# Attention with a ring of four PSUM banks for exponentials and three single banks for maxima

## The reference

```
xd = (layernorm(x) @ W_down).reshape(b, t, 16, 16)
keys, queries, values = per-head 16x16 products of xd     # keys and queries times 16 ** -0.25
dot  = einsum('bqhs,bkhs->bhqk', queries, keys)
attn = softmax(dot, axis=-1)
out  = einsum('bhqk,bkhs->bqhs', attn, values).reshape(b, t, 256) @ W_unify + b_unify
```

## Time and profile before

| | |
|---|---|
| runs shown | 2726.8, 2732.42, 2734.16 us; median 2732.42 |
| the profiled execution | 2731.22 us, span 2729.5 us, mean granted clock 0.979 |
| TensorE (PE) matmuls, weight loads (PEld) | 2627.3 us (96%), 1574.4 us (58%) |
| VectorE (DVE) | 2021.7 us (74%) |
| ScalarE (ACT) | 1761.2 us (65%) |
| GpSimd (POOL) | 917.5 us (34%) |
| attention steps | from about 647 to 2138 us of the span |

### The profile page before, as it was taken

One profiled execution on the slowest core, in us unless ns is written; L12 is line 12 of the kernel. 1 busy time (PEld: TensorE's weight loads), 2 busy tenths in 40 slices (PEclk: granted clock), 3 DMA queues, 4 the chain that ended last, 5 costly groups with the idle time before them and its releaser, 6 DMA issues. The chain is left out here.

```text
span 2729.5 us, 45612 instructions
## 1 busy us (share of the span) xinstructions
PE 2627.3 (96%) x17009; PEld 1574.4 (58%) x17009; DVE 2021.7 (74%) x3407; ACT 1761.2 (65%) x3314; POOL 917.5 (34%) x975
## 2 busy tenths in 40 slices
PE   6999999968999999999999999999999699999998
PEld 5888899953334334333343343343333388888998
DVE  5656547848898898897988988978997266665586
ACT  4444456734787887877877878878778344444576
POOL 2333334641332242423323322422212133332364
PEclk9999999986999999999999999999999699999999
DMA  4421214515144243242342442432421331321253
GB/s 116 100 70 56 62 52 137 156 53 101 48 85 85 55 96 66 65 99 52 77 105 51 90 80 54 81 65 65 84 68 32 107 86 57 76 70 32 86 160 96
DMA packets 191805, 216.79 MB, mean 79 GB/s; under 512 B 56364, under 2 KB 152804, under 8 KB 191584
## 3 DMA queue, kind: packets, MB, share of 16 engines
q1 hardware_dynamic: 156176, 169.03, 26.6%
q0 software_dynamic: 35408, 44.84, 5.8%
HBM read 114.54 MB, written 48.57 MB: 60 GB/s over the span
## 5 line engine op out<-in xcount | busy, mean ns | idle before, releaser
L1383 DVE TENSOR_REDUCE at_mxc<-at_pb 128x2 f32<-128x1024 f32 x1024 | 1217.7, 1222 | 185.2 <-PE at_pb L1208 178.4
L1316 ACT ACTIVATE at_ex<-at_pd 128x512 f32<-128x512 f32 x2048 | 1074.1, 603 | 328.9 <-PE at_pd L1219 325.1
L1219 PE MATMUL at_pd<-at_qa,at_ka 50*128 50x512 f32 x2048 | 616.2, 471 | 4.4 <-ACT at_ex L1316 4.4
L1219 PEld LDWEIGHTS at_pd<-at_qa,at_ka 50*128 50x128 f32 x2048 | 271.2, 186 | 570.8 <-issue 410.2
L699 ACT ACTIVATE f_ml_h<-f_ml_pL,b1T 128x512 f32<-128x512 f32 (+1 forms) x384 | 243.2, 633 | 480.2 <-PE f_ml_pL L763 458.7
L1228 PE MATMUL at_po<-at_ex,at_va 128*32 128x512 f32 x4096 | 551.5, 611 | 0.0
L614 DVE TENSOR_TENSOR f_ml_hl<-f_ml_h,f_ml_hh 128x512 fp32r<-128x512 f32 (+1 forms) x384 | 277.9, 724 | 368.0 <-ACT f_ml_hh L702 335.1
L1208 PE MATMUL at_pb<-at_ka,at_qa 48*128 48x512 f32 x2048 | 412.0, 447 | 21.6 <-DMA at_ka<-at_parts 11.3
L776 PE MATMUL f_ml_pA<-f_wh,f_ml_hh 128*128 128x256 f32 (+1 forms) x1408 | 411.4, 292 | 0.0
L778 PE MATMUL f_ml_pA<-f_wl,f_ml_hh 128*128 128x256 f32 (+1 forms) x1408 | 396.8, 282 | 0.0
L779 PE MATMUL f_ml_pA<-f_wh,f_ml_hl 128*128 128x256 f32 (+1 forms) x1408 | 396.7, 282 | 0.0
(11 more groups left out here) (123 smaller groups left out, 2642.0 us busy)
## 6 DMA issues: line engine op xcount, KB each, us to landing
f_wraw<-in_L_ffn_w SPq DMA_DIRECT2D x128, 256.0 KB, 2.9
at_qa<-at_parts SPq DMA_DIRECT2D x384, 64.0 KB, 2.5
at_ka<-at_parts SPq DMA_DIRECT2D x384, 64.0 KB, 2.7
at_oscr<-at_os POOLq DMA_DIRECT2D x63, 256.0 KB, 2.4
f_ml_xr<-in_L_attn_x SPq DMA_DIRECT2D x16, 512.0 KB
f_ml_xs<-in_L_attn_x SPq DMA_DIRECT2D x16, 512.0 KB, 4.6
x<-f_ml_yo SPq DMA_DIRECT2D x16, 512.0 KB, 6.2
at_xr<-x SPq DMA_DIRECT2D x16, 512.0 KB, 5.3
```

The source lines that it names most:

```text
L1219: eng.matmul(pd[n % RING][:, :], ka[g][rows, p, kt * P:(kt + 1) * P], qa[g][rows, qh, p, :], start=True, stop=True).then_inc(s_full.sem, 1)
L1316: eng.activation(ex[t % 2][:, j, :], pd[n % RING][:, :], ACT.Exp).then_inc(s_free[n % RING].sem, 1)
L1383: eng.tensor_reduce(mxc[:, t // NT, kh, t % NT::NT], pb[kh][:, :].rearrange("p (e k) -> p e k", e=2), AX.X, ALU.max, negate=True).then_inc ...
```

## The change

The two double banks for maxima become one tensor of MRING = 3 banks, and the ring of the exponentials gets the eighth bank: RING = 4. A maxima tile is now 128 queries x 512 keys of one head. It has a running number n (tile_of_max), uses bank n mod 3, waits for the read of tile n - 3, and has its own reduce of 512 numbers, so a step has four tiles and four reduces where it had two. TensorE's order within a step stays as it was (ORDER is 0, 1, 2, 3, and the e loops run where the pairs stood). The setup of the diagonals uses the first two of the three banks.

```diff
-RING = 3
+RING = 4
+MRING = 3
+ORDER = (0, 1, 2, 3)
...
-        pb = [ps(f"pb{i}", [P, T]) for i in range(2)]
+        pb = ps("pb", [P, MRING * 512])
         pd = [ps(f"pd{i}", [P, 512]) for i in range(RING)]
...
+        def tile_of_max(b, g, t, kh, e):
+            return 4 * (ST * unit(b, g) + t) + 2 * kh + e
+
+        def bank_of_max(n):
+            return pb[:, n % MRING * 512:(n % MRING + 1) * 512]
...
-            def for_max(b, g, t, kh):
+            def for_max(b, g, t, kh, e):
...
-                eng.wait_ge(s_mx.sem, s_mx.at(2 * (ST * unit(b, g) + t) + kh - 1))
-                for e in range(2):
-                    rows = slice(HALF * e, HALF * e + KROWS)
-                    mm = eng.matmul(pb[kh][:, e * NQ:(e + 1) * NQ], qa[g][rows, qh, p, qt * P:(qt + 1) * P],
-                                    ka[g][rows, p, kh * NQ:(kh + 1) * NQ], start=True, stop=True)
-                mm.then_inc(s_b.sem, 1)
+                n = tile_of_max(b, g, t, kh, e)
+                eng.wait_ge(s_mx.sem, s_mx.at(n - MRING + 1))
+                rows = slice(HALF * e, HALF * e + KROWS)
+                eng.matmul(bank_of_max(n), qa[g][rows, qh, p, qt * P:(qt + 1) * P],
+                           ka[g][rows, p, kh * NQ:(kh + 1) * NQ], start=True, stop=True).then_inc(s_b.sem, 1)
...
-                    for j in range(2 if tiles else 0):
-                        for_exp(self.ring, *coming, j, tiles[j])
-                    if ahead:
-                        for_max(*ahead, 0)
+                    for i in (0, 1) if tiles else ():
+                        for_exp(self.ring, *coming, ORDER[i], tiles[i])
+                    for e in range(2 if ahead else 0):
+                        for_max(*ahead, 0, e)
                     if a:
                         side_product(self.ring, a)
-                    if ahead:
-                        for_max(*ahead, 1)
-                    for j in range(2, GH if tiles else 2):
-                        for_exp(self.ring, *coming, j, tiles[j])
+                    for e in range(2 if ahead else 0):
+                        for_max(*ahead, 1, e)
+                    for i in (2, 3) if tiles else ():
+                        for_exp(self.ring, *coming, ORDER[i], tiles[i])
                     times_v(self.ring, b, par, g, t, done)
...
-            def maximum(b, g, t, kh):
-                eng.wait_ge(s_b.sem, s_b.at(2 * (ST * unit(b, g) + t) + kh + 1))
-                eng.tensor_reduce(mxc[:, t // NT, kh, t % NT::NT], pb[kh][:, :].rearrange("p (e k) -> p e k", e=2),
+            def maximum(b, g, t, kh, e):
+                n, c = tile_of_max(b, g, t, kh, e), t % NT + NT * e
+                eng.wait_ge(s_b.sem, s_b.at(n + 1))
+                eng.tensor_reduce(mxc[:, t // NT, kh, c:c + 1], bank_of_max(n),
                                   AX.X, ALU.max, negate=True).then_inc(s_mx.sem, 1)
```

More of the change, by code:

```diff
@@ L965, in attention @@
         norm = Norm(ctx, nc, k, "at_ln_", NT)
-        pb = [ps(f"pb{i}", [P, T]) for i in range(2)]
+        pb = ps("pb", [P, MRING * 512])
         pd = [ps(f"pd{i}", [P, 512]) for i in range(RING)]
         po = ps("po", [P, 512])
-        diagonals = Diagonals(ctx, nc, w, k, pb[0], xres[:, :, :])
+        diagonals = Diagonals(ctx, nc, w, k, pb[:, 0:2 * 512], xres[:, :, :])
         S = lambda n: Sem(ctx, nc, "at_" + n)
@@ L1198, in _ @@
                 s.open(eng)
-            def for_max(b, g, t, kh):
+            def for_max(b, g, t, kh, e):
                 qh, p, qt = t // NT, t % NT // 4, t % 4
-                if kh == 0 and (t == 0 or g == 0 and t == NT // 2):
+                if kh == 0 and e == 0 and (t == 0 or g == 0 and t == NT // 2):
                     eng.wait_ge(landed(g, p).sem, landed(g, p).at(loads(g, b + 1)))
-                eng.wait_ge(s_mx.sem, s_mx.at(2 * (ST * unit(b, g) + t) + kh - 1))
-                for e in range(2):
-                    rows = slice(HALF * e, HALF * e + KROWS)
-                    mm = eng.matmul(pb[kh][:, e * NQ:(e + 1) * NQ], qa[g][rows, qh, p, qt * P:(qt + 1) * P],
-                                    ka[g][rows, p, kh * NQ:(kh + 1) * NQ], start=True, stop=True)
-                mm.then_inc(s_b.sem, 1)
+                n = tile_of_max(b, g, t, kh, e)
[3 more added lines that the diff above has]
+                           ka[g][rows, p, kh * NQ:(kh + 1) * NQ], start=True, stop=True).then_inc(s_b.sem, 1)
             def for_exp(ring, b, g, t, j, n):
                 qh, kt, e, p = t // NT, t % NT, j % 2, j // 2
-                if kt == 0 and j == 0:
+                if kt == 0 and j == ORDER[0]:
                     eng.wait_ge(s_mr[qh].sem, s_mr[qh].at(16 * MLOADS * (unit(b, g) + 1)))
@@ L1283, in first @@
                         for kh in range(2):
-                            for_max(0, 0, t, kh)
+                            for e in range(2):
+                                for_max(0, 0, t, kh, e)
                 def lead(self, b, g, tiles):
-                    for j, n in enumerate(tiles):
+                    for j, n in zip(ORDER, tiles):
                         for_exp(self.ring, b, g, 0, j, n)
                 def step(self, b, par, g, t, coming, tiles, done, a, side, ahead, last):
-                    for j in range(2 if tiles else 0):
-                        for_exp(self.ring, *coming, j, tiles[j])
-                    if ahead:
-                        for_max(*ahead, 0)
+                    for i in (0, 1) if tiles else ():
+                        for_exp(self.ring, *coming, ORDER[i], tiles[i])
+                    for e in range(2 if ahead else 0):
+                        for_max(*ahead, 0, e)
                     if a:
                         side_product(self.ring, a)
-                    if ahead:
-                        for_max(*ahead, 1)
-                    for j in range(2, GH if tiles else 2):
-                        for_exp(self.ring, *coming, j, tiles[j])
+                    for e in range(2 if ahead else 0):
+                        for_max(*ahead, 1, e)
+                    for i in (2, 3) if tiles else ():
+                        for_exp(self.ring, *coming, ORDER[i], tiles[i])
                     times_v(self.ring, b, par, g, t, done)
@@ L1355, in lead @@
                 def lead(self, b, g, tiles):
-                    for j, n in enumerate(tiles):
+                    for j, n in zip(ORDER, tiles):
                         exponentials(self.ring, 0, j, n)
                 def step(self, b, par, g, t, coming, tiles, done, a, side, ahead, last):
-                    for j in range(2 if tiles else 0):
-                        exponentials(self.ring, t + 1, j, tiles[j])
+                    for i in (0, 1) if tiles else ():
+                        exponentials(self.ring, t + 1, ORDER[i], tiles[i])
                     if a:
                         side_out(self.ring, a)
-                    for j in range(2, GH if tiles else 2):
-                        exponentials(self.ring, t + 1, j, tiles[j])
+                    for i in (2, 3) if tiles else ():
+                        exponentials(self.ring, t + 1, ORDER[i], tiles[i])
                     if t % NT == NT - 1:
@@ L1388, in both_halves @@
                 h = half(b, g, qh)
-                eng.wait_ge(s_mx.sem, s_mx.at(2 * (ST * unit(b, g) + NT * (qh + 1))))
+                eng.wait_ge(s_mx.sem, s_mx.at(4 * (ST * unit(b, g) + NT * (qh + 1))))
                 eng.tensor_reduce(nm[:, qh, :], mxc[:, qh, :, :].rearrange("p k c -> p c k"), AX.X,
@@ L1476, in first @@
                         for kh in range(2):
-                            maximum(0, 0, t, kh)
+                            for e in range(2):
+                                maximum(0, 0, t, kh, e)
                         if t % NT == NT - 1:
@@ L1486, in step @@
                 def step(self, b, par, g, t, coming, tiles, done, a, side, ahead, last):
-                    if ahead:
-                        maximum(*ahead, 0)
+                    for e in range(2 if ahead else 0):
+                        maximum(*ahead, 0, e)
                     if t % NT == 3 and coming_half(t, g, last):
@@ L1492, in step @@
                         side_out(self.ring, a)
+                    for e in range(2 if ahead else 0):
+                        maximum(*ahead, 1, e)
                     if ahead:
-                        maximum(*ahead, 1)
                         if ahead[2] % NT == NT - 1:
```

## The result

The changed kernel takes 2930.11 us (median of 4 runs, 2928.76 to 2931.53), the kernel before 2732.09: ratio 1.0733, 95% interval 1.0714 to 1.0753, 198 us slower. 2922 was forecast.

The account below looks back on a forecast made before the run. The loop between ScalarE and TensorE was taken to bound plain steps at 2.60 us. Plain steps +202, sums' copy -4, xT and v +4, tail -13, first maxima +2 make +191: 2731 + 191 = 2922 us, range 2862 to 3040.

Parts of the forecast that it names:

- The bound of before: Plain attention steps: the ScalarE-TensorE loop closes each at 2.60 us; the wait for VectorE costs nothing.
- The fourth tile's wait: Plain steps: n+3 waits for the same step's read of n, so 2.605 becomes 3.17 us; 357 x 0.565 = +202.
- One sign: Profile after, plain steps: the fourth maxima tile's weight load idle some 0.7 to 0.9 us, released by VectorE's reduce.
- The price of a read of 512: VectorE's reduce of 128x512 from PSUM: taken as 0.69 us, between bounds of 611 and 692 ns.
- B: Plain steps: n+3 and j2 follow each other instead of running together, 357 x 0.23 = 82, 3004 us; chance 0.11.
- C: TensorE's granted clock drops in runs of plain steps; half of them at 5.1 us gives about 3266 us; chance 0.12.
- D: Plain steps: the wait for n costs nothing, steps some 2.47 us, not slower, 2668 us; chance 0.03.
- Side steps: Steps with side products: u, xd and qk unchanged; xT and v go from 3.10 to 3.17, 56 x 0.08 = +4.
- The copy of the sums: ScalarE's copy (L1322) at t=0 and t=8: hidden in the new loop, 48 x 0.09 = -4.
- The tail: Last 13 steps, without maxima: only the ring of four counts; -13 taken, -15 or, if the clock drops, about -5.
- The start: Beginning of the walk: +2 in the sum; low clock for up to eight steps longer, +12, in the range only.
- the first maxima: 13 walks on VectorE before any exponential: 2.43 instead of 2.28 us each, +2.

Follow-up runs that it names:

- three_tiles_ring3: Changed kernel without the fourth maxima tile of each step and with the exponentials' ring back at three: 2726.9 us, ratio to before 1.0026.
- split_only: Changed kernel with RING = 3 and MRING = 4 (four single maxima banks, reads of 512): 2724.2 us, ratio to before 0.9983.
- half_reads: Changed kernel with each maxima reduce reading only 256 of its tile's 512 columns: 2813.4 us, ratio to before 1.0304.
- two_banks: Changed kernel with two banks for maxima instead of three (MRING = 2): 3785.4 us, ratio to before 1.3863.
- fourth_after_exp: Changed kernel with only the fourth maxima tile moved behind j2 and j3 in TensorE's order: 2828.1 us (one run).

## Why the prediction was right

- *The bound of before.* It said that the loop j0, exponential, j3, product closes a plain step and the wait for VectorE is free. three_tiles_ring3 and split_only both show it.
- *The fourth tile's wait.* 3.17 us was worked out; from 700 us on 351 plain steps of the trace after, all but those of the tail, are 3.16 to 3.18. half_reads, two_banks and fourth_after_exp moved the step by what the chain gives (-0.26, +0.61, -0.22). One sign came out differently: the load of the fourth tile stands idle for 0.98, not 0.7 to 0.9, since it counts from the end of the load of n+2 at 0.53 of the step. That idle time is no link of the loop.
- *The price of a read of 512.* 0.69 taken, 683 ns measured. The table of the Trainium skill, VectorE: DVE Perf Modes, section on the TRN2 errata, gives an estimate of 658; the row decides against it by 25 ns. The slope between two reduces of the trace before (688) did better than halving a reduce of 1024 (611).
- *Rivals B, C and D.* n+3 and j2 start together (both at 1252.28), so B's 82 us did not come. The clock was 1.00 from 684.35 to 2310.93 us, so C did not come either; that was judged, not worked out, and it is in part luck: two_banks shows that a step 0.61 longer falls to C. D fell with the step of 3.17.
- *Side steps.* v at 3.17 and qk at 3.39 as said, u and xd unchanged. The copy of the sums no longer shows: the steps t=0 and t=8 are 3.17 like the others.
- *The tail.* The last eleven steps without a side product went from 36.9 us (2098.16 to 2135.10) to 22.8, the clock stayed at 1.00 and ScalarE is busy for 22.1 of them: -14, against -13 in the sum.
- *The start* was the term that was mis-sized: +2 in the sum, with +12 in the range. The clock rises later than before, at 685 us instead of 655: seven steps run at 0.50 and take 35.35 us, where the same seven took 20.9 before (649.16 to 670.07): +14.4. The sum had 4.3 for this stretch, +2 for the first maxima and 4 x 0.565 for plain steps, so it was 10 us short. The +2 itself did not delay the walk, which began at 649.0 instead of 649.16: the reads of the first maxima took 1.7 us longer but began 1.5 earlier.

The sum as measured: +198.5 from the eighth step to the tail (1626.6 us for 1428.1; the sum had some 200 for it), +14.4 at the start, -14.1 in the tail, 199 in all, for 197.5 in the spans (2927.0 and 2729.5). The 1.3 left lies outside these stretches and was not followed. So the forecast was low by 6.5 in the spans, and by 8 against the median: +10 at the start, less some 3.5 that was too high elsewhere.

## What to carry to other kernels

Count, for each ring of buffers, how many tiles an in-order engine issues between two runs of its long block, here the product with the values: one buffer fewer than tiles put a full round trip (write, read by the other engine, hand back) into every plain step, in both rings of this kernel. Taking a bank from one ring for the other only moved that round trip, so compare the two readers and what each ring's waiting tile holds up: here 0.60 on ScalarE with the product alone behind it gave 2.60, and 0.69 on VectorE, for a tile written later in the step (0.73 instead of 0.50) and with j2, j3 and the product behind it, gave 3.17. Which tiles stand where matters as much: the same three banks gave 3.17, 2.95 or 2.70 by the order on TensorE. Before a reorder, follow the chain of every tile, not only of the one that waits today.

## What was not expected of the hardware

The granted clock in two_banks: between 700 and 3167 us it fell to 1.2 GHz 19 times. It fell in or just behind plain steps of 3.78 us in which TensorE was busy for 2.89 (its matmuls stood 0.78 before the third tile of a step, on VectorE), and stayed low through steps of 5.61 us in which it was busy for 4.83. The changed kernel's steps, busy for 2.62 of 3.17, kept 2.4 GHz. Yet its first seven ran at 1.2 GHz: six of 5.0 us and one of 5.2, the first with a side product, at whose end the clock rose. Why it held in one kernel and fell in the other is not shown. The waits of two_banks thus cost more than their own length: it is 589 us above its expected time.

The Trainium skill, TensorE: Matmul & The Clock Gate, section "A second HAM failure mode: psum-queue depth-cycling", describes such a swing for a kernel that cycles through PSUM banks and in which TensorE idles briefly between groups. The trace of two_banks agrees with it (19 falls, mean clock 0.64), that of the changed kernel does not (1.00, though it too idles for 0.55 in each plain step).
